# A graph layer with experts: row work of each bucket moved into the edge gather loop, buckets in order of edge count

## The chip, the cores and the metric

The kernel runs on one core of a Trainium2 chip. The metric is the device time of one execution in microseconds, the median of several runs. All arithmetic is fp32 where nothing else is said.

## What is computed

Cut to what matters, N = 6250 nodes, 100,000 edges, D = 256, 16 experts, the best 2 of them for each node:

```python
xn  = layernorm(x)
agg = segment_sum(xn[dst] * edge_weight[:, None], src, N)      # rows gathered by dst, summed by src
h   = relu((xn + agg) @ W1 + b1) @ W2 + b2                     # 256 -> 512 -> 256
k, v = per-head norm of xn (8 heads); kv = k^T v / N           # over all nodes
x2  = x + h + xn @ kv + xn
xn2 = layernorm(x2)
val, idx = top_k(xn2 @ gate_w + gate_b, 2); w = softmax(val)
moe = sum over the 2 of w * (relu(xn2 @ w1[idx] + b1[idx]) @ w2[idx] + b2[idx])
out = x2 + layernorm(xn2 + moe) * gamma + beta
```

## The kernel before, in words

Nodes lie in NT = 49 buckets of 128 rows. The program is a string of blocks, and all engines meet at the end of each.

1. Sorting (line 484 on). Edges are counted by bucket and group of edges (28 groups), the counts rounded up to quads of four edges, and each quad gets an address. Buckets lie one after another in their natural order; `base` is the first quad of each, by a scan over `bucket_quads`. VectorE builds matrices for each group (`matrices`), TensorE and ScalarE turn them into records, and GpSimd scatters the records to DRAM, eight scatters a group (line 594). At the end tables are made that say, for each *part*, which tile of 128 sorted edges it takes and which bucket it adds to.
2. The gather loop (line 1029 on). There are ET = 816 tiles of 128 edges. GpSimd gathers 128 rows of `xn` for each with an indirect DMA (line 1137) into one of 24 places, three batches of eight. SP puts the indices of a batch in place once the batch that had these places before is used up (`stage`, waiting for a count of sums `s_sum`), and tells TensorE when a batch has landed (`landed`). A part is one tile for one bucket; a tile at a boundary is used by two, so there are more parts than tiles, ST = 864. For each part VectorE builds a 128x128 matrix of edge weights (`build`, line 1246), 12 parts ahead, TensorE multiplies it with the gathered rows (line 1161) into one of SUMB = 4 PSUM banks, and VectorE adds the sum to the bucket's rows in `xh` (`add`, line 1255). TensorE's sum c waits for VectorE's add c - 4. The loop body is a `pair` of 48 parts. Beside the parts run, in rounds 1 to 7, the head norms and the products of all 49 buckets, seven buckets a round (`heads`: VectorE at parts 12, 24, 36 and 48, TensorE's products ahead of parts 40 to 46); in round 8 the kv matrix is finished; in rounds 9 to 15 attention's product is added to the residual (`attention`).
3. The row stage (line 1459 on): 49 buckets, two a loop body, software-pipelined over seven steps with two sets of buffers. For each: copy of h, transposes, the hidden product (line 1529), ReLU (line 1591), the second product (line 1547), `x2` (line 1640), layer norm, `x2b` and `xn2` stored by SP, gate product, top two, and the rank of each choice among those for the same expert (`hot`, `place`, `slot2`). GpSimd turns the slots into indices and scatters the node ids with two indirect DMAs a bucket (`step`, lines 1495 to 1508); step t waits until step t - 2 has landed. SP loads w1 at the start and w2 piece by piece.
4. A short block (line 1736 on) makes tables for the experts' tiles. GpSimd reads the dispatched ids back (line 1746). Then come the experts' tiles, 114 of them, and the final norm.

The two lines of the scatter on which much rests are these:

```python
if over(half):
    pool.wait_ge(s_idst[p], half * (16 * TOPK))     # the step two before has landed
```

Of the kernel before, what the change touches and what calls it, by code (L numbers as in the profile page):

```python
# [18 lines left out]
I32 = mybir.dt.int32  # L19
# [39 lines left out]
def gps_layer(nc, x, src, dst, edge_weight, gW1, gb1, gW2, gb2, klw, klb, vlw, vlb,  # L59
# [32 lines left out]
    ST = -(-(ET + NT - 1) // (2 * ROUND)) * 2 * ROUND  # L92
    EROUNDS = ET // ROUND
    LSTEP = 4
# [25 lines left out]
    with ctx:  # L120
# [21 lines left out]
        def carver(region, size):  # L142
            at = [0]

            def carve(words):
# [54 lines left out]
        match = [a.bitcast(BF16) for a in (carve(GT * EC // 2),  # L200
                                           xh[:, sort_at + EC + NBG:sort_at + EC + 3 * NBG])]
        assert GT * EC // 2 <= 2 * NBG and GT * NGRP <= 512 and NR % 2 == 1
# [20 lines left out]
        edge_sel = carve(ROUND * P)  # L223
        rec_rows = edge_sel[:, 0:BT * P * REC].rearrange("p (c s w) -> p c s w", c=BT, w=REC)
        nd = carve(GT * D)
        sq = carve(GT * D)
# [3 lines left out]
        assert BT * P * REC <= GT * D and 2 * ST <= GT * D  # L230
# [35 lines left out]
        base = kvt[:, 0:NT]  # L266
# [10 lines left out]
        xT = [carve(D) for _ in range(2)]  # L277
# [4 lines left out]
        col_f = carve(EC // 2)  # L282
        landed_row = col_f.bitcast(I32)[0:1, 0:BT * P // LSTEP]
        release_row = col_f.bitcast(I32)[0:1, BT * P // LSTEP:BT * P // LSTEP + P]
        assert BT * P // LSTEP + P <= EC // 2
        col_f = col_f.bitcast(BF16)
# [3 lines left out]
        carve = carver(arena, AW)  # L290
        hin = [carve(D) for _ in range(2)]
        hT = [carve(D) for _ in range(2)]
        g1 = [carve(H) for _ in range(2)]
        x2 = [carve(D) for _ in range(2)]
        x2b = [carve(D) for _ in range(2)]
        xn2 = [carve(D) for _ in range(2)]
        xn2T = [carve(D) for _ in range(2)]
        beta_row = carve(D)
        hot = [carve(TOPK * NX).rearrange("p (k e) -> p k e", k=TOPK) for _ in range(2)]
        hot_both = [carve(NX // 2).bitcast(BF16) for _ in range(2)]  # L300
        hot_sum = [carve(NX // 2).bitcast(BF16) for _ in range(2)]
        place = carve(NX)
        hot_place = carve(TOPK * NX).rearrange("p (k e) -> p k e", k=TOPK)
# [56 lines left out]
        top_f = [sb(f"top_f{i}", [P, TOPK]) for i in range(2)]  # L360
        slot2 = [sb(f"slot2_{i}", [P, TOPK]) for i in range(2)]
# [6 lines left out]
        dest_all = sb("dest_all", [P, XT])  # L368
        b1_tile = sb("b1_tile", [P, FC * XT])
# [6 lines left out]
        mv2 = [sb(f"mv2_{i}", [P, 2]) for i in range(2)]  # L376
        std2 = [sb(f"std2_{i}", [P, 1]) for i in range(2)]
# [106 lines left out]
        with nc.Block() as block:  # L484
# [55 lines left out]
            def _(pool):  # L540
# [13 lines left out]
                pool.iota(ids_all, pattern=[[P, NT], [NTP, TOPK]], base=0, channel_multiplier=1,  # L554
# [172 lines left out]
            def _(dve):  # L727
# [66 lines left out]
                dve.tensor_tensor_scan(tiles_f[:], ones[:, 0:NT], bucket_quads[:, 0:NT], 0.0, ALU.mult, ALU.add).then_inc(s_dve, 1)  # L794
                dve.wait_ge(s_dve, n.add())
                dve.tensor_tensor(base, tiles_f[:], bucket_quads[:, 0:NT], ALU.subtract).then_inc(s_dve, 1)
# [112 lines left out]

                rounds(0)  # L910
                at0 = n.n
# [38 lines left out]
                then(dve.tensor_reduce(tile_bucket[:], past, AX, ALU.add))  # L950
                dve.tensor_scalar(tile_bucket_i[:], tile_bucket[:], float(NT - 1), None, ALU.min).then_inc(s_bk, 1)
                past_sum(tile_f, off_step)
                then(dve.tensor_tensor(tile_f, parts, tile_f, ALU.subtract))
# [58 lines left out]
        s_xT = sem("xn_transposed")  # L1012
        s_xTe = sem("xn_transpose_copied")
        s_att = sem("attention_rows")
        s_res = sem("residual_rows")
# [1129 lines left out]
```

## Time and profile before

| | us |
|---|---|
| median of the runs | 2666.47 (2661.55 to 2671.39) |
| span of the profiled execution | 2663.8 |
| sorting | 0 to 618 |
| gather loop | 618 to 1691 |
| row stage and reading back the ids | 1691 to 2028 |
| experts and end | 2028 to 2664 |

Busy over the whole span: TensorE 1707 us (64%), GpSimd 1611 (60%), VectorE 1534 (58%), ScalarE 644 (24%). No engine is busy throughout, so each stretch has to be read by itself: which engine is busy in it, and what the others wait for. The profiled execution is 2.7 us shorter than the median of the runs.

### The profile page before, as it was taken

How to read it: one execution, taken by the hardware profiler on the slowest of the kernel's cores; microseconds unless marked ns; L12 is line 12 of the kernel's file. 1: busy time of each engine (PE TensorE's matmuls, PEld its weight loads, DVE VectorE, ACT ScalarE, POOL GpSimd, SP SyncE). 2: the span in 40 equal slices, each digit the busy share in tenths (PEclk: the TensorE clock that was granted, in tenths of full speed). 3: DMA queues.
4: the chain of work that ended last, by engine and by line, in shares of the span. 5: the costliest groups of instructions: out<-in, count | busy, mean ns of one | idle time of the engine just before them, and what ended most of it. 6: DMA issues, size and time to landing. Idle time of an engine off the chain costs nothing. (4 is left out here: it accounts for less than half of the span.)

```text
span 2663.8 us, 42526 instructions
## 1 busy us (share of the span) xinstructions
PE 1707.0 (64%) x8895; PEld 1423.3 (53%) x8896; DVE 1534.1 (58%) x4251; ACT 643.5 (24%) x1976; POOL 1610.9 (60%) x1802
## 2 busy tenths in 40 slices
PE   6406666624566666565566665798853999999900
PEld 2106666623455555454455454687843888888800
DVE  8598555534776666776566665365542343344477
ACT  4607555510000000000000000244421333333322
POOL 8006888876777777777777777033433555555535
PEclk9758777765678877878788877798976999999955
DMA  4001000134433333334443334643331111111175
GB/s 144 0 0 30 17 16 16 30 3 128 131 114 115 116 114 114 115 105 122 125 118 117 117 106 99 170 75 62 67 62 52 61 61 61 59 63 61 57 219 174
DMA packets 159628, 227.50 MB, mean 85 GB/s; under 512 B 51782, under 2 KB 118916, under 8 KB 159519
## 3 DMA queue, kind: packets, MB, share of 16 engines
q0 software_dynamic: 60816, 138.87, 18.7%
q1 hardware_dynamic: 85934, 74.74, 10.8%
q10 hardware_dynamic: 12768, 12.85, 1.5%
q14 instruction: 92, 0.75, 0.1%
q8 instruction: 18, 0.29, 0.1%
HBM read 182.97 MB, written 42.96 MB: 85 GB/s over the span
## 5 line engine op out<-in xcount | busy, mean ns | idle before, releaser
L1137 POOL DMA_INDIRECT lower<-xn_rows,lower x816 | 804.2, 986 | 254.6 <-issue 248.1
L1161 PE MATMUL bank<-lower 128*128 x1728 | 592.6, 503 | 387.9 <-SPq L1062 283.0
L1161 PEld LDWEIGHTS bank<-lower 128*128 128x128 f32 x1728 | 424.2, 258 | 528.3 <-issue 450.8
L1255 DVE TENSOR_TENSOR xh<-xh,bank 128x256 f32 x864 | 363.8, 421 | 289.9 <-PE bank L1161 283.7
L594 POOL DMA_INDIRECT edge_records_sorted<-lower x224 | 308.1, 1375 | 221.8 <-ACT lower L705 153.8
L1246 DVE TENSOR_SCALAR lower<-iota_n,lower 128x128 f32<-128x128 f32 x864 | 315.0, 366 | 87.0 <-issue 83.7
L638 PE MATMUL bank<-lower 128*64 128x128 f32 x1568 | 227.8, 319 | 112.8 <-ACT lower L689 110.1
L638 PEld LDWEIGHTS bank<-lower 128*64 128x64 f32 x1568 | 221.6, 167 | 117.4 <-DVE lower L893 110.8
L1861 POOL DMA_INDIRECT expert_rows<-arena,dest_idx x114 | 114.7, 1006 | 198.0 <-DVE arena L1957 187.2
L1891 PEld LDWEIGHTS bank<-arena 128*128 128x128 f32 x1824 | 223.6, 193 | 6.6 <-issue 0.8
L1948 DVE TENSOR_SCALAR arena<-bank,b_tile 128x128 f32<-128x128 f32 x456 | 128.4, 344 | 170.3 <-PE bank L1891 170.3
L1891 PE MATMUL bank<-arena 128*128 128x128 f32 x1824 | 224.3, 277 | 0.4 <-ACT arena L1929 0.4
L1912 PE MATMUL bank<-upper,arena 128*128 x912 | 223.8, 388 | 0.1
L689 ACT ACTIVATE lower<-lower 128x32 f32<-128x32 f32 x784 | 169.3, 309 | 123.6 <-DVE lower L878 123.3
L1912 PEld LDWEIGHTS bank<-upper,arena 128*128 128x128 f32 x912 | 163.9, 189 | 30.2 <-issue 6.4
L1929 ACT ACTIVATE arena<-lower 128x1024 f32 x114 | 120.5, 1057 | 61.0 <-issue 61.0
L1869 POOL DMA_INDIRECT arena<-xn_rows,tok_idx x114 | 109.5, 960 | 40.4 <-issue 33.4
L1107 ACT ACTIVATE arena<-bank 128x256 f32<-128x256 f32 x49 | 18.8, 384 | 458.8 <-PE bank L1186 458.8
L1506 POOL DMA_INDIRECT dispatched_ids<-slot_id,slot_idx x98 | 94.5, 964 | 53.8 <-POOL slot_id L1502 34.1
L1957 DVE COPY arena<-bank 128x256 f32<-128x256 f32 x114 | 48.4, 425 | 132.7 <-PE bank L1912 132.7
L1501 POOL CAST slot_idx<-slot 128x2 uint32<-128x2 f32 x49 | 9.7, 198 | 175.9 <-issue 77.0
L1529 PE MATMUL bank<-arena,upper 128*128 128x128 f32 x784 | 112.1, 302 | 3.5 <-ACT arena L1598 3.4
(290 smaller groups left out, 2330.5 us busy)
## 6 DMA issues: line engine op xcount, KB each, us to landing
lower<-xn_rows,lower POOLq DMA_INDIRECT x816
arena<-xn_rows ACTq DMA_DIRECT2D x14, 896.0 KB, 5.5
lower<-in_L_ffn_w SPq DMA_DIRECT2D x1, 8192.0 KB, 26.3
xn_rows<-xh SPq DMA_DIRECT2D x7, 896.0 KB, 4.2
x_plus_beta<-arena SPq DMA_DIRECT2D x49, 128.0 KB
xn_rows<-xh SPq DMA_DIRECT2D x49, 128.0 KB
upper<-in_x SPq DMA_DIRECT2D x1, 6144.0 KB
upper<-in_L_ffn_w SPq DMA_DIRECT2D x12, 512.0 KB
```

The source lines that it names most:

```text
L594: pool.indirect_dma_start(rec_dram, bass.IndirectOffsetOnAxis(quad_idx[i][:, c:c + 1], 0), quads[i][:, c * QW:(c + 1) * QW], None).then_in ...
L638: mm = pe.matmul(bank[6 + p][0:NQ * QW, 0:P], moving[p][:, e].rearrange("p c w -> p (c w)"), row_hot[p][:, e, :], start=e == 0, stop=e == ...
L689: done = act.activation(moving[p][:, e, :, 1], col_hot[p][:, e, :], ACT.Copy, scale=group_wgt[p][:, e:e + 1])
L1137: pool.indirect_dma_start(edge_rows[:, q * GB + c, :], None, xn_dram, bass.IndirectOffsetOnAxis(gath_idx[q].bitcast(U32)[:, c:c + 1], 0)). ...
L1161: pe.matmul(bank[c % SUMB][:, 0:D], edge_sel[:, c % ROUND, :], rows_flat[:, ds(places[c % GB] * D, D)], start=True, stop=True).then_inc(s_ ...
L1246: dve.tensor_scalar(edge_sel[:, c % ROUND, :], iota_n[:], lane[:, ds(t, 1)], weight_s[:, ds(t, 1)], ALU.is_equal, ALU.mult).then_inc(s_sel, 1)
L1255: dve.tensor_tensor(xh[:, at], xh[:, at], bank[c % SUMB][:, 0:D], ALU.add).then_inc(s_acc, 1)
L1861: pool.indirect_dma_start(y_dram, bass.IndirectOffsetOnAxis(dest_idx[p][:], 0), yrow[p], None).then_inc(s_yst[p], 16)
L1891: mm = pe.matmul(bank[2 + p][:, m * P:(m + 1) * P], w1_tile[p][:, c * F + m * P:c * F + (m + 1) * P], tokT[p][:, c * P:(c + 1) * P], start ...
L1912: mm = pe.matmul(bank[6 + p][:, 0:D], hidT[p][:, m * P:(m + 1) * P], upper[:, ds(e * (FC * D) + m * D, D)], start=False, stop=m == FC - 1)
L1929: act.activation(w1_tile[p], lower[:, ds(e * (DC * F), DC * F)], ACT.Copy).then_inc(s_w1t, 1)
L1948: dve.tensor_scalar(hidT[p][:, m * P:(m + 1) * P], bank[2 + p][:, m * P:(m + 1) * P], b1_tile[:, ds(t + m * XT, 1)], 0.0, ALU.add, ALU.max ...
```

## The change

- Sorting: buckets get a key of edge quads x 64 + their number, and a rank among these keys by comparing all with all (49x49). Their quads are laid out in rising order of count. After the first four groups, `bucket_order` works out which bucket stands at each place, and prepares the ids' table with it.
- The loop's body becomes a round of PER = 18 parts, and ST = 49 x 18 = 882. As buckets stand in rising order of size, the bucket at place s is complete when 18(s + 1) parts are added. SUMB becomes 3, `landed` is looked at every 3 parts, bucket and place numbers are loaded 6 at a time, matrices are built 9 parts ahead in 18 buffers. The heads' work of rounds 1 to 7 now lies beside 18 parts (VectorE at parts 1, 3, 6, 9 and 18, with the bias add of the residual in it; TensorE ahead of parts 11 to 17).
- The row stage as a block is gone. Its work is a `slot`, with one set of buffers: TensorE's `turn`, `hidden`, `second` (with attention's product added in PSUM), `turn_xn2`, `gate` and `ranks`, VectorE's `residual`, `norm`, `choose` and `placed`, and ScalarE's copies, ReLUs and root, which now also issues the load of xn and both stores. Rounds 9 to 16 hold two slots each, rounds 17 to 48 one, and the last slot runs after the loop.
- The slots of all buckets are kept in `slot_all`. The scatter of the ids is the same `step`, now at the start of the block that follows, before the ids are read back. w1 and w2 (8 MB each) are loaded at the start of that block too.

```diff
-    ST = -(-(ET + NT - 1) // (2 * ROUND)) * 2 * ROUND
+    PER = 18
+    ST = NT * PER
-    LSTEP = 4
+    LSTEP = 3
+    LB = 6
...
+                dve.tensor_tensor(by_bucket, bucket_key.unsqueeze(2).to_broadcast([P, NT, NT]),
+                                  bucket_key.unsqueeze(1).to_broadcast([P, NT, NT]), ALU.is_gt).then_inc(s_dve, 1)
...
+                dve.tensor_reduce(bucket_rank, by_bucket, AX, ALU.add).then_inc(s_dve, 1)
...
                 rounds(0)
+                bucket_order()
...
-        SUMB = 4
+        SUMB = 3
...
+                def slot(s):                                   # ScalarE
+                    b = bucket(s)
+                    act.wait_ge(s_acc, s * PER + PER)
+                    act.activation(hin, xh[:, ds(b * D, D)], ACT.Copy).then_inc(s_hin, 1)
+                    act.wait_ge(s_hT, s + 1)
...
+                    act.activation(hxT, bank[3][:, 0:2 * D], ACT.Copy).then_inc(s_hTe, 1)
...
+                def hidden(s):                                 # TensorE
+                    pe.wait_ge(s_hTe, s + 1)
...
+                def second(s):
+                    pe.wait_ge(s_gr, s * HC + HC)
...
+                ALONE = (0, 3, 6, 9, 12)
+                FIRST, OTHER = (0, 2, 4, 7, 8), (9, 11, 13, 16, 17)
...
+                with pe.Fori(TWO_FROM + 1, ONE_FROM) as r:
+                    two = (r - TWO_FROM) * 2
+                    parts(r, slot(two, FIRST) | slot(two + 1, OTHER))
+                with pe.Fori(ONE_FROM, NT) as r:
+                    parts(r, slot(r - 1, ALONE))
...
+                ALONE = (1, 7, 8, 13)                          # VectorE
+                FIRST, OTHER = (1, 5, 6, 9), (10, 14, 15, PER)
...
             @block.gpsimd                                      # the block after the loop
             def _(pool):
+                def step(j, k):
...
+                run_steps(pool, step, 0, NT - 1, 1, (NT - 1) // 2)
+                for p in range(2):
+                    pool.wait_ge(s_idst[p], 16 * TOPK * ((NT + 1 - p) // 2))
                 pool.wait_ge(s_block, 1)
```

## Rows read from the trace of the kernel before

**Rows 1.** Busy time by stretch: us and instructions of each engine, clock, DMA

```profile
618.00:1691.00 1073.00, 675.66 (x2329) 522.59 (x2327) 692.76 (x1898) 33.94 (x70) 804.15 (x816) 0.77 0.40 113
1691.00:2028.00 337.00, 249.75 (x1669) 226.81 (x1669) 158.61 (x897) 127.57 (x442) 110.51 (x196) 0.86 0.37 83
2028.00:2664.00 636.00, 469.58 (x3083) 418.12 (x3083) 297.64 (x922) 195.29 (x293) 322.43 (x485) 0.88 0.29 91
```

Columns of the above: stretch, its length, then TensorE matmul, weight load, VectorE, ScalarE and GpSimd.

**Rows 2.** Groups of instructions, gather loop: busy and mean, idle before with releaser

```profile
L1137 POOL DMA_INDIRECT lower<-xn_rows,lower x816 | 804.2, 986 | 254.6 <-issue 248.1 <-DMA lower<-lower 6.5
L1161 PE MATMUL bank<-lower 128*128 x1728 | 592.6, 503 | 387.9 <-SPq L1062 283.0 <-DVE lower L1246 54.8 <-DVE xh L1255 49.1
```

**Rows 3.** By line: duration min, median and max in ns, first and last start

```profile
L1137 POOL DMA_INDIRECT lower<-xn_rows,lower x816: 941/946/2737, 618.0 to 1670.2; - x164
...
L1255 DVE TENSOR_TENSOR xh<-xh,bank x864: 406/422/423, 632.1 to 1690.4; 128x256 f32 x173
...
L1506 POOL DMA_INDIRECT dispatched_ids<-slot_id,slot_idx x98: 954/960/1181, 1729.8 to 2010.5; - x98
```

**Rows 4.** GpSimd in order of time, end of the scatter: start, us, instruction

```profile
1999.11 0.18 POOL L1501 CAST slot_idx<-slot 128x2 uint32<-128x2 f32 x1 [3.10 <-DMA dispatched_ids<-slot_id,slot_idx]
...
2001.48 0.96 POOL L1506 DMA_INDIRECT dispatched_ids<-slot_id,slot_idx  x1 [0.30 <-DMA dispatched_ids<-slot_id,slot_idx]
...
2008.10 0.18 POOL L1501 CAST slot_idx<-slot 128x2 uint32<-128x2 f32 x1 [1.92 <-issue]
```

**Rows 5.** Waits in the row stage: who waited for whom, us, times, longest

```profile
DVE slot L1675 <- POOL slot_id L1502: 48.2, 20, 5.9
...
POOL slot_idx L1501 <- DMA dispatched_ids<-slot_id,slot_idx: 39.3, 16, 5.3
...
DVE arena L1640 <- issue: 3.0, 3, 1.2
```

**Rows 6.** VectorE in order of time, first parts of a heads round

```profile
816.97 0.35 DVE L1246 TENSOR_SCALAR lower<-iota_n,lower 128x128 f32<-128x128 f32 x1 [4.23 <-issue]
...
818.52 0.42 DVE L1255 TENSOR_TENSOR xh<-xh,bank 128x256 f32 x1
...
819.15 0.42 DVE L1255 TENSOR_TENSOR xh<-xh,bank 128x256 f32 x1
...
822.79 0.35 DVE L1246 TENSOR_SCALAR lower<-iota_n,lower 128x128 f32<-128x128 f32 x1 [0.48 <-issue]
...
825.52 2.01 DVE L1280 TENSOR_REDUCE arena<-arena 128x56 f32<-128x1792 f32 x1
...
829.82 0.34 DVE L1246 TENSOR_SCALAR lower<-iota_n,lower 128x128 f32<-128x128 f32 x1
```

**Rows 7.** TensorE in order of time, sums between the products of the heads

```profile
866.19 0.59 PE L1161 MATMUL bank<-lower 128*128 x2
...
867.50 0.59 PE L1161 MATMUL bank<-lower 128*128 x2
```

**Rows 8.** Groups of instructions, row stage

```profile
L1529 PE MATMUL bank<-arena,upper 128*128 128x128 f32 x784 | 112.1, 302 | 3.5 <-ACT arena L1598 3.4
...
L1547 PE MATMUL bank<-upper,arena 128*128 128x256 f32 x392 | 94.1, 383 | 0.0
...
L1591 ACT ACTIVATE arena<-bank,gb_col 128x128 f32<-128x128 f32 x196 | 56.0, 369 | 29.5 <-PE bank L1529 22.8 <-remote 4.8
```

**Rows 9.** GpSimd in order of time, during the centring of a heads round

```profile
828.13 2.59 POOL L1137 DMA_INDIRECT lower<-xn_rows,lower  x1 [0.30 <-issue]
```

**Rows 10.** VectorE and GpSimd in order of time, sorting

```profile
117.39 1.59 DVE L810 TENSOR_TENSOR upper<-xh 128x1372 f32<-128x1372 f32 x1
...
119.12 2.66 DVE L815 TENSOR_TENSOR xh<-xh,upper 128x1372 f32<-128x1372 f32 x1
...
219.04 1.44 POOL L594 DMA_INDIRECT edge_records_sorted<-lower  x1 [153.84 <-ACT lower L705]
...
257.06 0.17 DVE L903 CAST lower<-lower 128x8 uint32<-128x8 f32 x1 [8.31 <-DMA edge_records_sorted<-lower]
```

More of the change, by code:

```diff
@@ L1120, in _ @@
                 heads(NG - 1)
-                with act.Fori(0, NG - 1) as g:
-                    attention(g)
-                attention(NG - 1)
+                act.wait_ge(s_kv, DC)
+                act.dma_start(beta_row, row(beta)).then_inc(s_beta, 16)
+                load_xn(bucket(0))
+                slot(0)
+                with act.Fori(1, NT - 1) as s:
+                    slot(s)
+                slot(NT - 1)
+                act.wait_ge(s_x2st, 16 * NT)
+                act.wait_ge(s_xn2st, 16 * NT)
             @block.gpsimd
@@ L1208, in _, with slot @@
+                def slot(s, places):
+                    steps = turn, hidden, second, turn_xn2, gate
+                    return {c: [lambda f=f: f(s)] for c, f in zip(places, steps)}
+                ALONE = (0, 3, 6, 9, 12)
+                FIRST, OTHER = (0, 2, 4, 7, 8), (9, 11, 13, 16, 17)
                 pe.wait_ge(s_srec, 16 if ET % P == 0 else 32)
@@ new lines, in norm @@
+                def norm(s):
+                    if over(s):
+                        dve.wait_ge(s_x2st, s * 16)
+                    dve.tensor_tensor(x2b, x2, beta_row, ALU.add).then_inc(s_x2b, 1)
+                    dve.wait_ge(s_std2, s + 1)
+                    then(dve.reciprocal(rstd2[:], std2[:]))
+                    if over(s):
+                        dve.wait_ge(s_xn2k, s)
+                        dve.wait_ge(s_xn2st, s * 16)
+                    dve.tensor_scalar(xn2, x2, mv2[:, 0:1], rstd2[:], ALU.subtract, ALU.mult).then_inc(s_xn2, 1)
+                    dve.wait_ge(s_xn2, s + 1)
@@ new lines, in _, with slot @@
+                bucket_now = [None]
+                per_slot = 9
+                def slot(s, places, last=True):
+                    steps = [lambda: placed(s - 1)] if over(s) else [lambda: None]
+                    steps += [lambda: residual(s), lambda: norm(s), lambda: choose(s)]
+                    return {c: [f] for c, f in zip(places, steps)}
+                ALONE = (1, 7, 8, 13)
+                FIRST, OTHER = (1, 5, 6, 9), (10, 14, 15, PER)
+                constants()
+                parts(TWO_FROM, slot(0, FIRST) | slot(1, OTHER))
@@ new lines, in _ @@
+                with dve.Fori(TWO_FROM + 1, ONE_FROM) as r:
+                    n.enter(r - TWO_FROM - 1, 2 * per_slot)
+                    two = (r - TWO_FROM) * 2
+                    parts(r, slot(two, FIRST) | slot(two + 1, OTHER))
+                    n.leave(ONE_FROM - TWO_FROM - 1)
+                with dve.Fori(ONE_FROM, NT - 1) as r:
+                    n.enter(r - ONE_FROM, per_slot)
+                    parts(r, slot(r - 1, ALONE))
+                    n.leave(NT - 1 - ONE_FROM)
+                parts(NT - 1, slot(NT - 2, ALONE))
@@ L1450, in gps_layer @@
+                placed(NT - 2)
+                residual(NT - 1)
+                norm(NT - 1)
+                choose(NT - 1)
+                placed(NT - 1)
+        s_w1 = sem("w1_loaded")
+        s_w2 = sem("w2_loaded")
         s_ids = [sem(f"ids_staged{i}") for i in range(2)]
         s_idst = [sem(f"ids_landed{i}") for i in range(2)]
[L1453 to L1456 removed]
```

684 lines of the change are left out of this document (278 added, 406 removed).

## Prediction, as recorded before the changed kernel was measured

> **What bounds the kernel now.** I read the busy time by stretch first [rows 1]. The program is a string of blocks: sorting the edges (0 to 618 us), the gather loop (618 to 1691), the row stage (MLP, norm, gate, ids; 1691 to 2028 where the first dispatched ids are read back), and the experts and the end (636 us), which the change doesn't touch. In the gather loop GpSimd is the busiest engine: 816 indirect gathers [rows 2]. One takes 0.946 us, the gap behind it 0.30, so 1.25 us [rows 2, 3], and 816 of them 1020 us of the 1073. The rest is mostly 21 gathers of up to 2.7 us, each under a 2 us VectorE operation on 1792 elements, like the one of 2.59 us at 828 [rows 9]. So this loop waits for gathers, and VectorE and TensorE have room.
>
> The row stage isn't what its engines suggest. TensorE is busy 250 of 337 us, but GpSimd's scatter of the ids sets the pace: VectorE waits 48 us for it before overwriting a slot buffer, and GpSimd itself waits for landings [rows 5]. A step (two casts, two scatters) waits until the step two before it has landed. The step at 2008.10 follows the scatter issued at 2001.48 by 6.62 us, and the same parity's step at 1999.11 by 8.99 us [rows 4]. Nothing else was moving then, so 4.5 us a bucket is the scatter's own pace; 49 of them are 220 us. This is the row to keep in mind: the change moves this scatter out from behind the work it ran beside.
>
> **The change, part by part.** *Sorting.* Before the first scatter of edge records at 219.04 VectorE has no pause, so what is added there counts in full [rows 10]. Two comparisons or products over 49x49 = 2401 elements and a third, and two reductions over as many: an operation of 1372 elements took 2.66 us there with transposed operands and 1.59 without, and 1792 elements took 2.01 in the loop [rows 6, 10]; so about 2.7 each, four of them, 11 us with the small ones. The second group (`bucket_order`, 10 us) comes where VectorE later waits 8.31 us for a landing [rows 10]; I leave 5 us of it, also for GpSimd held up by long VectorE operations, and 1 for the tables. Sum +17 (bounds 11 and 22).
>
> *The row stage goes away, the scatter stays.* From 337 us to: 220 for 49 steps with nothing beside them, about 20 because 16 MB of weights now load in the first part of it, 7 for the last landing. That is 247, a gain of 90 only. Bounds: 3.33 us a step if no landing were waited for (2.37 us from cast to second scatter plus 0.96) [rows 4], 163 + 27 = 190; and the pace of before with traffic beside it, (2008.10 - 1729)/48 = 5.8 a step, 285 + 7 = 292, where the 1729 is the first scatter [rows 3].
>
> The Trainium skill (DMA: Bandwidth & Descriptors, Anatomy of one DMA — SWDGE (gpsimd) path) gives such a transfer a fixed cost of about 2.0 us, most of it the write receipt. By that the landing would be in time and the step would cost what its issue costs, 163 us in all; the trace's 6.62 us doesn't agree, and the measurement decides.
>
> *The gather loop.* Its VectorE and TensorE now have to do, per 18 parts, what the rows below say, while GpSimd needs for the 17 tiles behind them 17 x 1.25 = 21.2 us (25.1 in a round with three held gathers). The engines are in order and coupled: TensorE may be three sums ahead of VectorE's adds, so a wait on one side soon stops the other. Costs, each from a row:
> - a part, when data lies ready: 819.15 - 818.52 = 0.63 us on VectorE [rows 6]; 18 are 11.3. Register loads 0.48 and more, three a round, 1.5 [rows 6].
> - a heads round (7). Its VectorE work was spread over 48 parts and now has 18: bias add 2.0, centring 829.82 - 825.52 = 4.3, squares 2.0, scaling 2.9, adding up 0.9: 12.1. Eleven parts 7.0, loads 1.0. The last seven parts each stand behind TensorE's products of the heads: 867.50 - 866.19 = 1.31 a part [rows 7], 9.2. Sum 29.3.
> - a bucket's row work. VectorE was busy 158.6/49 = 3.2 us for a bucket [rows 1]; its 17 operations now each wait for the one before (0.06, an estimate), and a register load: 4.7. TensorE and ScalarE: hidden product 112.1/49 = 2.3, four ReLUs 56.0/49 = 1.14, second product 94.1/49 = 1.9 [rows 8], attention about 0.6 (four of hidden's sixteen). These 5.9 us are serial, with a single set of buffers, and TensorE's sums queue behind them.
> - a round with one bucket (32). 11.3 + 1.5 + 4.7; the bucket's last add, ScalarE's copy, four transposes and the first sum before VectorE adds again, 2.1 idle; adds held behind hidden and second product (5.9 and two sums against four adds, `placed` and a load), 2.4. Sum 22.0, against GpSimd's 21.2. No cover is left.
> - a round with two buckets (8): 11.3 + 1.5 + 9.4 + 2 x 3.1 (now only two parts stand between the products) + 2 x 1.7 (after `choose` TensorE does ranks and transposes before the next sum). Sum 32.
>
> Chain from 618: 44 until the first round and the bias split are done (as before, but the adds no longer catch up), 7 x 29.3 = 205, the round with the kv matrix 20, waiting for beta 4, 8 x 32 = 256, 32 x 22 = 704, the last bucket alone 16. That is 1249 against 1073, +176. Behind a late add waits the release of a gather buffer on SP, and behind that GpSimd: three batches of eight tiles let it run ahead once, not every round. Bounds: +38 if GpSimd sets the pace all along (18 more parts and the last bucket, 22 + 16), and +280: a bucket round at 24.5 and a double one at 36, since the clock was 0.77 of full speed in this loop [rows 1] and the products of a bucket were priced at 0.86.
>
> *Sum* against the profiled execution: 2664 + 17 + 176 - 90 = 2767. The median of the runs is 2.7 us above that execution's span, so 2770.
>
> **Rivals.** *The gather still sets the pace.* For it: VectorE's own work is 17.5 of 21.2 us in most rounds, GpSimd is the bound now, and a few us can be absorbed. Against: the double and heads rounds exceed 21 by VectorE's work alone. Time 2664 + 17 + 38 - 90 = 2629, which is not slower. It decides if a round of one bucket stays under 21.2 us and the 15 others lose little.
>
> *The scatter is issue-bound.* For it: in steps without other waits GpSimd goes on after 3.33 us. It decides if landings take under 6.66 - 2.37 = 4.3 us after the second scatter. Against: 6.62 in a quiet stretch. Time 2770 - 57 = 2713. The skill's rule above leads here.
>
> *Each turn of the loop costs 4 us.* At every turn of the 48-part loops VectorE stood 4.2 us with nothing to wait for [rows 6], hidden so far. There were some 12 such turns; now there would be 45, 190 us, and the time 2960. Against: in the row stage, a loop of shorter body, VectorE's issue gaps before its first operation reach only 1.2 us [rows 5], and 18 parts with two buckets are shorter than 48 parts with one group. The Trainium skill (Runtime: NRT & Kernel Launch, Instruction fetch mechanics) says that a taken branch stalls when its target is outside the current two-page window. By it the shorter body would be free, the trace agrees as far as these rows go.
>
> **How the numbers follow.** My forecast 0.70, with its own range 2700 to 2870. The gather keeping the pace 0.14 (2620 to 2700). Issue-bound scatter with a bound loop 0.05. The 4 us turns 0.06. Gather keeping the pace and a short scatter together, 2572: 0.05. The range of 2640 to 2870 leaves out the last two, a part of the second, and little of the first. More than 2% away from before, about what a measurement can tell from no change, is under 2613 or over 2720. Faster 0.06; same 0.20 (second case, third case, edge of the first); slower 0.74.
>
> **What would show it.** Right: GpSimd's gathers no longer 1.25 us apart in the first third of the loop, idle before a gather on a landing of its index batch; the last gather at 1830 or later instead of 1670; ScalarE's last bucket near 1885; casts of the scatter alternating 3.3 and 5.7 us for 220 to 260 us with the other engines idle. Wrong: the last gather near 1690; double rounds under 26 us; a scatter step of 3.3; VectorE idle on issue of 4 us in each round. The single weakest term is the round with one bucket: 1 us there is 32 us.

## The result, and the profile after

The changed kernel takes **3030.3 us** (3028.6 to 3032.1) against 2666.5: 1.136 times the time before, 95% interval 1.130 to 1.142. In a second sitting it was 3065.6 against 2709.3, 1.132 (1.127 to 1.138). The forecast was 2770 with a range of 2640 to 2870: the direction was right, the size was not.

First the same table by stretch as [rows 1], of the kernel after: sorting, gather loop with the row work in it, the block that scatters the ids, and the rest. The columns are the start and end, the length, busy us of each engine with instructions, the granted clock of TensorE, DMA share and GB/s.

```profile
core 0: us, PE busy (x) PEld busy (x) DVE busy (x) ACT busy (x) POOL busy (x), PEclk, DMA share, GB/s
0.00:632.00 632.00, 315.08 (x1817) 258.94 (x1819) 405.52 (x552) 286.88 (x1171) 375.59 (x306) 0.73 0.15 33
632.00:2117.00 1485.00, 1020.75 (x4031) 774.71 (x4030) 884.93 (x2818) 169.01 (x462) 798.54 (x816) 0.77 0.32 90
2117.00:2390.00 273.00, 1.30 (x6) 0.71 (x6) 4.23 (x21) 1.53 (x2) 109.30 (x196) 0.50 0.34 62
2390.00:3030.00 640.00, 469.84 (x3079) 418.24 (x3079) 295.59 (x914) 195.16 (x292) 322.64 (x485) 0.88 0.28 87
```

Against [rows 1] that is +14 for sorting, +412 for the loop, 337 turned into 273, -64, and +4 for the rest. The forecast had +17, +176, -90 and 0. So nearly all of the error, 236 of 263 us, is in one term, the loop. No engine is full in it: TensorE is busy 69% of the stretch, VectorE 60%, GpSimd 54%.

The page's group of the gathers shows that they no longer set the pace; compare the idle time before them in [rows 2]. The two sources after it are the register loads of VectorE and TensorE (min/median/max in ns; the columns otherwise as in [rows 3]).

```profile
L1231 POOL DMA_INDIRECT lower<-xn_rows,lower x816 | 798.5, 979 | 620.2 <-DMA lower<-lower 385.3
```

```profile
L1395 DVEq TENSOR_LOAD <-upper x147: 805/1071/1558, 637.5 to 2091.2; - x147
L1242 PEldq TENSOR_LOAD <-arena x147: 824/1470/1848, 634.5 to 2089.3; - x147
```

GpSimd stands still for 385 us waiting for its index batches, which SP stages only when sums have released a buffer. The same load in the kernel before was this:

```profile
L1262 DVEq TENSOR_LOAD <-upper x108: 593/598/854, 623.6 to 1684.8; - x108
```

**The loop round by round**, measured from the first add of a round to that of the next, against the working on record:

| part of the loop | forecast | measured |
|---|---|---|
| until the second round's first add | 44 | 46.0 |
| 7 heads rounds | 7 x 29.3 = 205 | 7 x 30.9 = 216.5 |
| round with the kv matrix, waiting for beta | 24 | 21.5 |
| 8 rounds with two buckets | 8 x 32 = 256 | 8 x 39.0 = 311.9 |
| 32 rounds with one bucket | 32 x 22.0 = 704 | 869.9 (27.2 each) |
| last bucket | 16 | 19.6 |

The one-bucket round is 166 of the 236 us that were missed, the two-bucket round 56, the heads 11. Below, "one-bucket round" is the mean of 29 of the 32 (27.3 here) and "two-bucket round" the mean of six of the eight (39.2), which leaves out the first and the last of each kind.

Where a one-bucket round changes over, in order of time, VectorE, TensorE and ScalarE (GpSimd's and part of the weight loads' lines are left out):

```profile
1770.30 0.42 DVE L1388 TENSOR_TENSOR xh<-xh,bank 128x256 f32 x1
1770.86 0.42 ACT L1178 ACTIVATE lower<-xh 128x256 f32 x1 [9.48 <-DVE xh L1388]
...
1771.33 0.57 PE L1287 MATMUL bank<-ident,lower 128*128 128x128 f32 x2 [1.46 <-ACT lower L1178]
...
1771.69 0.63 PE L1290 MATMUL bank<-ident,lower 128*128 128x128 f32 x2
...
1772.43 0.35 DVE L1379 TENSOR_SCALAR lower<-iota_n,lower 128x128 f32<-128x128 f32 x1 [1.71 <-issue]
...
1773.26 2.92 PE L1255 MATMUL bank<-lower 128*128 x6 [0.94 <-DVE lower L1379]
...
1774.62 0.42 DVE L1388 TENSOR_TENSOR xh<-xh,bank 128x256 f32 x1 [1.84 <-PE bank L1255]
...
1778.89 1.47 PE L1255 MATMUL bank<-lower 128*128 x6
```

The last add of a bucket (1770.30) starts ScalarE's copy; TensorE stood waiting for the copy, transposes, then does its own register load (0.83 us) and the first sum, and only at 1774.62 does VectorE add again: 4.3 us from add to add, where two adds are 0.63 apart with data ready [rows 6]. One of VectorE's own register loads, 1.42 us, lies inside these 4.3. The three sums take 2.92 us here, at a granted clock of 0.50 of full speed (the 1.2 GHz level) after TensorE's wait, and 1.47 a few us later at 1.00 (2.4 GHz), after the 3 us of the hidden product.

The row of waits for VectorE over those 29 rounds (1256.6 to 2048.0; us, times, longest) says how the time is spent beside its 16.1 us of work a round:

```profile
DVE xh L1388 <- PE bank L1255: 168.9, 168, 3.1
DVE lower L1379 <- issue: 99.1, 87, 1.7
DVE lower L1554 <- issue: 12.8, 29, 0.4
```

That is 5.8 us a round for sums, and 3.4 us without a releaser at the builds, 87 times in 29 rounds. Three register loads stand in each round, and at 0.82 and 1.41 us in turn they are 3.35. So that idle time is the loads. The other 1.9 us of the 27.3 are short gaps between dependent operations, a further register load (0.44) among them.

### The profile page after: what moved, and what is told of

Its sections match the earlier page's. It is cut to its first block and busy times, and to the rows that moved or that the text cites. A ratio compares the mean times of both kernels' runs of the same rounds, so it can differ in the third digit from the quotient of the medians.

```text
span 3030.3 us, 43604 instructions
## 1 busy us (share of the span) xinstructions
PE 1807.0 (60%) x8931; PEld 1452.6 (48%) x8932; DVE 1590.3 (52%) x4303; ACT 652.6 (22%) x1927; POOL 1606.1 (53%) x1802
## 5 line engine op out<-in xcount | busy, mean ns | idle before, releaser
L1255 PE MATMUL bank<-lower 128*128 x1764 | 632.2, 496 | 209.1 <-DVE lower L1379 81.7
L1255 PEld LDWEIGHTS bank<-lower 128*128 128x128 f32 x1764 | 390.7, 241 | 355.8 <-issue 298.7
L1388 DVE TENSOR_TENSOR xh<-xh,bank 128x256 f32 x882 | 371.1, 421 | 324.4 <-PE bank L1255 321.6
L1867 ACT ACTIVATE arena<-bank 128x256 f32<-128x256 f32 x114 | 43.8, 384 | 553.3 <-PE bank L1833 553.2
L1297 PEld LDWEIGHTS bank<-lower,upper 128*128 128x128 f32 x784 | 145.6, 276 | 9.7 <-ACT lower L1182 1.1
L1297 PE MATMUL bank<-lower,upper 128*128 128x128 f32 x784 | 139.1, 353 | 0.7 <-ACT lower L1182 0.7
```

The source lines that it names most:

```text
L1255: pe.matmul(bank[c % SUMB][:, 0:D], edge_sel[:, c % ESEL, :], rows_flat[:, ds(places[c % LB] * D, D)], start=True, stop=True).then_inc(s_s ...
L1297: mm = pe.matmul(bank[4][:, m * P:(m + 1) * P], gW1_sb[:, c, m * P:(m + 1) * P], hxT[:, c * P:(c + 1) * P], start=c == 0, stop=c == DC - 1)
L1388: dve.tensor_tensor(xh[:, at], xh[:, at], bank[c % SUMB][:, 0:D], ALU.add).then_inc(s_acc, 1)
```

## The experiments

All are variants of the changed kernel, or of the kernel before, and each ran beside the kernel before on one chip, in one sitting. Sittings differ: the median of the kernel before was 2666, 2700, 2709, 2668 and 2668 us in five of them (2709 and the last 2668 on one and the same chip, at different times) and 2979 in a sixth. So totals are compared as ratios, or by their rounds. The loop without row work, the two banks, the doubled hidden product and the kernel before repeated were executed once each, so they are read by their rounds and stages alone. The changed kernel repeated is the measure for that:

> The changed kernel itself, unchanged, as the measure for its variants on one chip: 3025 to 3060 us, 1.12 to 1.145 times the kernel before.

It took 3065.6 us; its one-bucket round was 27.29 and its two-bucket round 39.3, as at first. Its ids block and the sorting are what is longer. So round times can be compared between these sittings, the sixth left out.

### The loop without row work

```diff
-                with pe.Fori(ONE_FROM, NT) as r:
-                    parts(r, slot(r - 1, ALONE))
+                with pe.Fori(TWO_FROM, NT) as r:
+                    parts(r)
+                ...
+                with pe.Fori(1, NT) as s:
+                    for f in (turn, hidden, second, turn_xn2, gate):
+                        f(s)
```

> The changed kernel with the row work taken out of the gather loop: the loop sums the buckets in the new order, in rounds of 18 tiles, and the MLP, norm and gating of the 49 buckets run one after another behind it. What it tells is the time of a round without row work, and the length of one bucket's chain alone. Theory A (the row work on VectorE and TensorE is what a round of the changed kernel waits for): rounds without it take 21.6 to 23.5 us, which is 17 to 18 gathers at 1.25 plus the register loads, against 27.3; so 4 to 6 us a round are the price of one bucket's row work. Rival B (the loop itself is slower in rounds of 18 with loads of 6, the row work costs little): rounds without row work take 25 us or more. A bucket's chain alone: 14 to 18 us, so the total is near 3030 - 170 + 49 x 16 = 3640.

The total is 3516.7 us; a round took 21.6 us. The group of the gathers over those rounds (1110 to 1737):

```profile
L1231 POOL DMA_INDIRECT lower<-xn_rows,lower x499 | 473.8, 950 | 152.1 <-issue 152.1
```

No gather waits for anything: 1.25 us each, as before. So rounds of 18, new order and slow loads all fit under GpSimd, and the row work alone is what lengthens a round, by 5.7 us for one bucket and 17.6 for two. Theory A holds. Summing the buckets in another order costs these rounds nothing by itself. A bucket's chain alone, behind the loop, takes 16.3 us, as expected; the total stayed under the 3640 expected because the loop lost 326 us and not 170.

### The register loads

```diff
-                                place_row[0:1, ds(r * PER + c, LB)]
+                                place_row[0:1, ds(r * (PER // LB * 8) + c // LB * 8, 8)]
```

(the same for `bucket_row`, and the tables are laid out so by their DMAs)

> The changed kernel with the two tables of the register loads laid out in places of 8: each load of VectorE and of TensorE takes 8 values from a 32-byte aligned address, as in the kernel before, in place of 6 values from 24-byte steps. Nothing else differs in what is computed. Theory A (the loads, in series with the adds on both engines, made the gather loop longer than the sum): each load takes 0.60 us instead of 0.82 and 1.41 to 1.47, which is 1.5 us a round on each engine; 49 rounds x 1.5 = 75 us off the changed kernel if one engine's loads are in series, 150 off if both are. Rival B (the loads lie beside other waits, and the surplus is in dependent operations and a slow TensorE): less than 20 us off. Rival C (the address does not matter, the number of values does): the loads of 8 take 1.5 us or more, and the total does not fall.

```profile
L1400 DVEq TENSOR_LOAD <-upper x147: 594/600/866, 644.4 to 2049.5; - x147
L1247 PEldq TENSOR_LOAD <-arena x147: 587/595/971, 641.3 to 2048.2; - x147
```

Eight aligned values load in 0.60 us, less than six unaligned ones, so it isn't their number. 3020.2 us against 3065.6 in the same sitting, -45. The one-bucket round went from 27.3 to 26.05, the two-bucket round only from 39.3 to 38.9. That is between A and B: 1.25 of the 1.5 us that one engine saves, and nothing for the second. Over the same 29 rounds VectorE's idle time at the builds fell from 99.1 to 56.1 us, 1.48 a round, and its waits for sums rose from 168.9 to 175.8, 0.24 a round. So the loads of the two engines stand beside each other, not in series.

### The turn of the bucket

```diff
-                ALONE = (0, 3, 6, 9, 12)
+                ALONE = (2, 5, 8, 11, 14)
```

(and VectorE's places from 1, 7, 8, 13 to 3, 9, 10, 15)

> The changed kernel, but in a round with one bucket its five steps on TensorE stand before parts 2, 5, 8, 11, 14 and VectorE's before 3, 9, 10, 15, instead of 0, 3, 6, 9, 12 and 1, 7, 8, 13. So the first two sums of a round no longer stand behind the bucket's copy on ScalarE and its transposes. Theory A (the turn of the bucket, 4.3 us from the last add of a round to the first sum's add in the trace, is an idle of both engines that this place makes): 1 to 2 us a round off, 31 rounds, the total 30 to 60 us under the changed kernel's. Rival B (the engines are full, the wait only moves to a later place): less than 0.5 us a round, total within 15 us.

2939.2 us, ratio 1.102 (1.099 to 1.104) against 1.136: -91 us. The one-bucket round is 24.5, 2.8 less, more than theory A gave, and VectorE's waits for sums in 29 rounds fell from 168.9 to 79.9 us, 3.1 a round. The two sums ahead of the turn are enough:

```profile
1250.03 0.67 PE L1287 MATMUL bank<-ident,lower 128*128 128x128 f32 x2
1250.23 0.42 DVE L1388 TENSOR_TENSOR xh<-xh,bank 128x256 f32 x1
...
1250.86 0.42 DVE L1388 TENSOR_TENSOR xh<-xh,bank 128x256 f32 x1
1250.91 1.93 PE L1255 MATMUL bank<-lower 128*128 x6
...
1252.12 0.42 DVE L1388 TENSOR_TENSOR xh<-xh,bank 128x256 f32 x1 [0.58 <-PE bank L1255]
```

VectorE adds at 1250.23 and 1250.86 while TensorE transposes and goes on to the next sums; its wait for a sum in these rows is 0.58, where it was 1.84 behind a wait of 1.71.

This could be the place among the parts, or the dependence on the bucket finished an instant ago. The next one keeps the places and takes the dependence away:

```diff
-                    parts(r, slot(r - 1, ALONE))
+                    parts(r, slot(r - TWO_FROM, ALONE))
```

(one bucket a round, finished nine rounds before; the last nine follow the loop one by one)

> The changed kernel, but every round from the ninth on takes one bucket, the one finished nine rounds earlier, and the nine last buckets come one after another behind the loop. The steps stand at the same parts (0, 3, 6, 9, 12 and 1, 7, 8, 13). Theory A (in the changed kernel the first sum of a round stands behind the copy and the transposes of the bucket whose last add has just been made; 2.8 us of a round are this dependence): with a bucket that is long finished such a round takes 24.0 to 25.0 us at the old places, as it did with the later places. Rival B (the place of the steps among the parts mattered, not the dependence): 26.5 to 27.5. The nine buckets alone take 14.9 us each, 134, against the 8 rounds with two buckets that go, 8 x (39 - 24.5) = 116; total by A 2945 to 2965, by B 3030 to 3060 (a chip like the first).

> One bucket a round, finished nine rounds earlier, the steps at the old parts, once more, on a chip where the landings of gathers don't hold the loop. Theory A (2.8 us of a changed kernel's round are the wait for the bucket just finished): rounds with one bucket take 24.0 to 25.0 us. Rival B (the place of the steps among the parts mattered, not the dependence): 26.5 to 27.5.

The first of these ran, like three others below, in the sitting where the kernel before took 2979 us. Transfers came late there all through the loop: GpSimd waited 488 us for its index batches, up to 20 at a time, against 155 us in the run of the same kernel below, and its rounds took 25 to 42 us. Which transfer was late first I did not settle. Its 3277.9 us against 2979.4 (1.103) tells nothing of the dependence. The second ran in a sitting like the others: 2933.2, ratio 1.099, and every one-bucket round took 23.1 to 24.7 us, 23.9 in the mean, at the old places. VectorE's waits for sums in 29 rounds are 71.2 us instead of 168.9, 3.4 a round. So it is the dependence: 3.4 us of a round were the wait for the bucket just finished and the slower products behind it.

TensorE's clock follows. The rows are the one-bucket rounds of the changed kernel, of the turn made later, and of the bucket of nine rounds before, with the same work in each:

```profile
1256.60:2048.00 791.40, 564.22 (x2205) 428.87 (x2204) 467.97 (x1596) 91.06 (x261) 466.95 (x493) 0.80 0.35 96
```

```profile
1250.20:1961.60 711.40, 519.11 (x2210) 390.87 (x2209) 463.17 (x1597) 91.66 (x262) 469.70 (x495) 0.84 0.39 107
```

```profile
1134.90:1827.30 692.40, 502.60 (x2206) 379.58 (x2205) 463.88 (x1595) 91.06 (x261) 468.68 (x495) 0.88 0.39 110
```

The same 2205 products keep TensorE busy 564, 519 and 503 us, at a granted clock of 0.80, 0.84 and 0.88. VectorE's busy time stays at 464 to 468. A part of what a wait costs is that the products behind it run at the lower clock, as the 2.92 us against 1.47 for three sums showed.

### Is TensorE in series?

```diff
-                    for m in range(HC):
+                    for m in (*range(HC), *range(HC)):
```

(the hidden product of each bucket is done twice into the same bank)

> The changed kernel with the hidden product of each bucket done twice into the same bank (16 more matrix products of 128x128 a bucket, the result is the same). They take 2.6 us in the loop's trace. Theory A (a bucket's products on TensorE are in series with the sums, no slack is left there): rounds with one bucket 29.7 to 30.0 instead of 27.3, with two 44 instead of 39, and the total grows by 110 to 130 us. Rival B (VectorE is what a round waits for, TensorE has slack): less than 1 us a round, total +40 at most.

The total is 3131.0 us. One-bucket round 29.2, +1.9; two-bucket round 44.4, +5.1. Against the 2.6 us that theory A took for the added product this looks like three quarters in the one and all in the other. But the added work has to be read from the trace: the hidden product's busy time grew by 62.2 us in 29 one-bucket rounds, 2.1 each, and by 25.3 in six two-bucket rounds, 4.2 each, where the sums also got slower (granted clock 0.73 instead of 0.76). So the product is nearly wholly in series in both. That is A, though 29.2 lies just under its 29.7.

```diff
-        SUMB = 3
+        SUMB = 2
```

> The changed kernel with two PSUM banks for the sums of parts in place of three, so TensorE can be two sums ahead of VectorE's adds. Theory A (VectorE's idle time on sums, 5.7 us of a 27.3 us round with one bucket, is sums held behind a bucket's products, and the depth of the banks covers part of each hold): each of the four holds in a round shows one add more, 0.6 to 1 us each, so such a round takes 29.5 to 31 us and the total grows by 70 to 120 us. Rival B (the depth does not matter, both engines are simply full): under 0.5 us a round, total within 20 us.

The total is 3127.0 us. One-bucket round 29.9, +2.6; two-bucket round 39.9, +0.7. For one bucket the lead of TensorE over the adds covers part of each hold, as A says: VectorE's waits for sums in 29 rounds grew from 168.9 to 237.8 us, 2.4 a round. How much of that is the lead alone isn't shown, because the granted clock fell from 0.80 to 0.73 with it and TensorE's busy time grew by 2.5 us a round. For two it hardly matters, so another thing rules there.

### The two-bucket round

In the trace of the three edits together (next part) I read the waits over six such rounds, 12 buckets:

```profile
DVE xh L1392 <- PE bank L1259: 72.1, 47, 2.5
...
PE bank L1318 <- DVE lower L1573: 37.7, 12, 3.4
PE bank L1283 <- DVE lower L1590: 28.7, 12, 2.6
```

Each engine waits for the other in turn. For each bucket TensorE waits 3.1 us at its fourth step (transposing xn2) for VectorE's norm, and 2.4 us at the ranks for VectorE's choice of the bucket before, though it is only the *next* bucket's transposes that are held there. That one can be moved:

```diff
                 def turn(s):
-                    if over(s):
-                        ranks(s - 1)
                 ...
                 def hidden(s):
+                    if over(s):
+                        ranks(s - 1)
```

(VectorE reads the ranks two or three parts later)

> The kernel with the three edits together (aligned loads, scatter without waits, bucket's steps two parts later), and one edit more: TensorE does the ranks of the bucket before with the next bucket's hidden product instead of ahead of its transposes, and VectorE reads them two parts later. Theory A (a round with two buckets, 38.6 us, is a chain that goes back and forth between TensorE and VectorE; 2.5 us of TensorE's idle time stand twice in it at the ranks, which wait for the choice of the bucket before): 3 to 5 us off each of the 8 rounds, 25 to 40 in all. Rival B (such rounds are full on TensorE's side, the wait moves): less than 1 us a round.

> The three edits together and the ranks done with the next hidden product, once more on another chip. Theory A (the ranks' wait for the choice of the bucket before stands twice in the chain of a two-bucket round): these rounds take 34 to 36 us instead of 38.6. Rival B (the wait moves): 37.5 or more.

In the sitting with late transfers 3113.5 against 2979.4 (1.047), undecided. In the other 2741.6, ratio 1.029 (1.026 to 1.032), against 1.035 for the three edits without it. The one-bucket round is 23.5 there, 0.5 longer; the two-bucket round went from 38.9 to 35.1, and the wait at the ranks is gone from the answer; the one for the norm stands:

```profile
DVE xh L1392 <- PE bank L1259: 48.8, 40, 3.5
...
PE bank L1318 <- DVE lower L1573: 37.6, 12, 3.4
```

So A holds for these rounds, 3.9 us off where it gave 3 to 5, but about half of the gain is lost again in the 32 one-bucket rounds, and the total fell by less than the 25 to 40 us it gave. 3 us still part 35.1 from the forecast's 32. The waits for the norm, 3.1 us twice a round, are more than that; whether they are the cause was not tried.

### The edits together

> The changed kernel with three edits together: loads of 8 aligned values, the ids scattered without waits for landings, and the bucket's steps two parts later in rounds with one bucket. Theory A (each acts on its own stretch, so the gains add up): 45 + 120 + 30 to 60 off, a total of 2800 to 2870, 1.035 to 1.06 times the kernel before, which it does not reach. Rival B (the loop falls back to the gather's pace once loads and turn are mended, 21.4 us a round): 2700 or less.

The total is 2759.0 us, ratio 1.035 (1.032 to 1.037), 271 us under the changed kernel. One-bucket round 23.0: the loads' 1.25 and the turn's 2.8 add up, as A says. The total lies between A's range and B's, 41 us under A, since A had put the turn at 30 to 60 us and it gave 91 alone. The gather's pace of 21.4, rival B, isn't reached.

> One bucket a round, finished nine rounds earlier, with aligned loads, the scatter without waits and the ranks done with the next hidden product. Theory A (with the turn's wait and the slow loads gone a round is near the gather's pace of 21.4 us): rounds of 21.4 to 22.5 us and a total of 2700 to 2740, still above the kernel before. Rival B (the bucket's products keep 1.5 us a round above the gather): rounds of 23 and a total of 2750 to 2770.

> One bucket a round, finished nine rounds earlier, with aligned loads, the scatter without waits and the ranks done with the next hidden product, once more on another chip. Theory A (with the turn's wait and the slow loads gone a round is near the gather's pace of 21.4 us): rounds of 21.4 to 22.5 and a ratio of 1.01 to 1.03 to the kernel before. Rival B (the bucket's products keep a round 1.5 us above the gather): rounds of 23 and a ratio of 1.03 to 1.04.

In the sitting with late transfers 3175.5 (1.066). In the other 2748.0, ratio 1.030 (1.028 to 1.033), with rounds of 22.7 (VectorE's first place is 4 in both, not 1): one us above the loop without row work, between the theories and nearer to B.

### The scatter of the ids

```diff
-                    if over(half):
-                        pool.wait_ge(s_idst[p], half * (16 * TOPK))
-                    pool.tensor_copy(slot_idx[p][:], slot_all[:, ds(t * TOPK, TOPK)])
+                pool.tensor_copy(slot_i[:], slot_all)
+                for j in range(NJ):
+                    pool.indirect_dma_start(..., IndirectOffsetOnAxis(slot_i[:, j:j + 1], 0), ids_all[:, j:j + 1], None)
```

> The changed kernel with the ids scattered at once: one cast of all slots, then the 98 indirect DMAs one behind the other with no wait for those before, from columns that stay. Theory A (each pair of steps waits for two landings, so the wait is the bound of the block): what is left is GpSimd's issue, near 1.26 us each as for the gathers, 98 x 1.26 = 124 plus about 15 for the last landing; the block goes from 273 to about 145 and the total to about 2900. Rival B (the DMA rings work off such scatters one behind the other at the pace seen, 2.4 us each quiet and 3.9 beside the weights): the block stays over 230 and the total over 2990.

```profile
2129.20 0.96 POOL L1662 DMA_INDIRECT dispatched_ids<-arena,dest_all  x1 [0.30 <-issue]
2130.46 0.95 POOL L1662 DMA_INDIRECT dispatched_ids<-arena,dest_all  x1 [0.30 <-issue]
...
2266.08 1.15 POOL L1667 DMA_INDIRECT arena<-dispatched_ids,arena  x1 [18.54 <-DMA dispatched_ids<-arena,dest_all]
```

Scatters follow each other every 1.26 us and the block, from the cast to the reading back, takes 142.7 us instead of 273: 2909.7 us, ratio 1.077 (1.075 to 1.080). Theory A. The queue takes scatters 1.26 us apart even beside the weights. The edit also takes away the two casts of each step and the wait for them, and a step with these and without a wait for landings takes 3.3 us [rows 4]. So of the 4.76 us of a quiet step 1.4 were the wait for landings, of the 7.7 us beside the weights 4.4, and 0.8 us of each step were the casts.

> The changed kernel, but the two big weight loads wait for the end of the ids scatter. Theory A (the loads of 16 MB stretch each landing while they last: 7.7 us a step against 4.76 after them): all 49 steps take 4.8, the scatter ends after 235 us in place of 267, and the expert stage then waits some 48 us for its first weights; the total moves by +5 to +25 us (3035 to 3055). Rival B (the first steps were slow for another reason, as the code's first passes): the first 12 steps stay at 7.7 us, and the total is 3070 or more.

The weight loads now wait for the scatter's end. The cast of the first bucket, of the 13th and of the 49th, in the changed kernel:

```profile
2117.75 0.19 POOL L1665 CAST slot_idx<-node_all 128x2 uint32<-128x2 f32 x1 [72.99 <-POOLq L1097]
...
2210.07 0.19 POOL L1665 CAST slot_idx<-node_all 128x2 uint32 x1 [0.51 <-DMA dispatched_ids<-slot_id,slot_idx]
...
2381.57 0.19 POOL L1665 CAST slot_idx<-node_all 128x2 uint32<-128x2 f32 x1 [0.47 <-DMA dispatched_ids<-slot_id,slot_idx]
```

and with late weights:

```profile
2123.86 0.19 POOL L1667 CAST slot_idx<-node_all 128x2 uint32<-128x2 f32 x1 [72.06 <-POOLq L1097]
...
2190.50 0.19 POOL L1667 CAST slot_idx<-node_all 128x2 uint32 x1
...
2379.72 0.18 POOL L1667 CAST slot_idx<-node_all 128x2 uint32<-128x2 f32 x1
```

The first 12 steps took 7.7 us each beside the weights and 5.55 without them, the 36 others 4.76 and 5.26, which is the sitting (the changed kernel repeated had 8.5 and 5.2 in its own). So the weights make a step some 3 us longer while they load. Total 3067.7, ratio 1.136: the steps came out as A says, though slower by the sitting, and the total above its 3055. Weights that start later cost what the scatter gains.

### The kernel before without these waits

> The kernel before, with only the waits of its own ids scatter on the landings of two tiles earlier taken away, by a place of its own for each tile's slots. Theory A (the row stage of the kernel before, 337 us, was itself paced by the scatter's landings, 5.8 us a tile beside TensorE's 4.5): the stage takes about 54 steps x 4.5 = 245 us, and the total is 2570 to 2590. Rival B (the stage is paced by the chain through four engines, the scatter runs beside it): within 15 us of 2666.

> The kernel before without the scatter's waits on landings once more, on the chip of the runs beside it. Theory A (the scatter's landings pace its row stage wherever it runs, and how much depends on the chip): 15 to 50 us less than the kernel before, which makes it the fastest of all. Rival B (the first gain was of that one chip): no difference beyond 0.3%.

2654.2 us, ratio **0.983** (0.980 to 0.986), and in the sitting with late transfers 2939.6, ratio 0.985 (0.980 to 0.991). This version beats both kernels, by a little under 2%. One of the two casts of a step went with the waits, so the gain isn't of the waits alone. The gain of 46 us is half of what A said: with the scatter out of the way the row stage takes 5.4 us a bucket, not TensorE's 4.5. GpSimd now waits for VectorE's slots, 99 us in 260, so another engine sets the pace; which link of its chain does I did not settle. The kernel before, profiled again in another sitting, shows that the gain depends on that:

> The kernel before itself, unchanged, for a profile from the chip on which the runs beside it are made. Both theories: the same stages as in its first profile within 1.5%.

```profile
1742.19 1.01 POOL L1506 DMA_INDIRECT dispatched_ids<-slot_id,slot_idx  x1 [0.84 <-POOL slot_id L1502]
...
2051.84 0.95 POOL L1506 DMA_INDIRECT dispatched_ids<-slot_id,slot_idx  x1 [0.30 <-issue]
```

First to last scatter 309.7 us here. By [rows 3, 4] it was about 280 at first; without the waits it was this:

```profile
1740.41 1.04 POOL L1500 DMA_INDIRECT dispatched_ids<-arena,dest_all  x1 [0.44 <-POOL dest_all L1497]
...
2000.01 0.96 POOL L1500 DMA_INDIRECT dispatched_ids<-arena,dest_all  x1 [0.30 <-issue]
```

That is 259.6 us. So 20 to 50 us of the row stage were waits for landings, the cast included. The profiled kernel before took 2712.0 us, as in the other runs of that sitting.

## Why the prediction was wrong, step by step

- **The bound of the kernel before** was read rightly: 1.25 us a gather sets the loop's pace, and it does so again (21.6 us a round) once the row work is out. The scatter's landings did hold the row stage, as [rows 5] said, but what was hidden behind them was 5.4 us a bucket rather than 4.5.
- **Sorting**, +17: measured +14.
- **The row stage leaves, the scatter stays**, -90: measured -64. The mechanism was right. The term mis-sized is a step beside the weights, 7.7 us where the sum had 4.5 and 20 us for all of them (12 steps, +18), and 4.76 for the quiet pair's 4.5 (36 steps, +9).
- **The loop**, +176: measured +412. The failed step is "a round with one bucket, 22.0". By VectorE's time, over the 29 rounds:

  | in a one-bucket round | in the sum | measured |
  |---|---|---|
  | VectorE's own work | 11.3 + 3.2 = 14.5 | 16.1 |
  | gaps between a bucket's operations, and its register load | 1.5 | 1.9 |
  | the three register loads of the parts | 1.5 | 3.4 |
  | idle until a sum is there | 2.1 + 2.4 = 4.5 | 5.8 |
  | all | 22.0 | 27.3 |

  The loads were priced at 0.5 each from a row of the kernel before, where eight aligned values were loaded; six values at 24-byte steps took 0.82 and 1.41, and aligning them gave 1.25 us a round back. The turn of the bucket was given 2.1 us, added up as single operations. It holds both engines at once for 4.3 us (a register load included), leaves TensorE at the lower clock, and empties the lead of sums that would have covered the next product; moving it gave 2.8 us back, taking the dependence away 3.4. No variant tested the first two rows, 2.0 of the 5.3 us, and no run shows the 0.06 us by which one operation was said to wait for the one before. The loads and the moved turn together bring the round from 27.3 to 23.0, but these 4.3 us are not all error, since 2.1 us for the turn were in the 22.0. The rounds of 23.0, and of 22.7 in the best variant, stay 1 us and more over the 21.6 without row work; what makes that up is open.
- **The bounds.** 24.5 us for such a round was meant for the clock alone and was too low, and with it the upper end of the range; by its own terms, 2.5 us in 32 rounds and 4 in 8, that end adds up to +288 and not +280. The lower end, +38, counted 22 us for 18 more parts at the gather's pace, though 816 gathers stay 816. In a sum of VectorE's work plus idle pieces each wait that is not foreseen only adds.
- **A round with two buckets, 32**: measured 39. The sum put the products behind VectorE's work and saw one direction of waiting. In fact the chain of a bucket goes from one engine to another fifteen times, and in a two-bucket round both engines wait in turn. 3.9 us were TensorE waiting at the ranks for the choice, in order in its queue ahead of work that was ready; the rest of the 7 stays open.
- **Heads rounds**, 29.3: measured 30.9, 5% off; no variant tested their terms.
- **Rivals.** *The gather still sets the pace*: false as the change stands, GpSimd waits 385 us; true without row work. *The scatter is issue-bound*: false, a step took 4.76 and more; it becomes true when nothing waits, 1.26 us apiece. In the trace of the changed kernel a scatter landed 1.8 us after its issue at the least, 6.3 in the median and 16.9 at the most. The rule of the Trainium skill that I weighed there (DMA: Bandwidth & Descriptors, Anatomy of one DMA — SWDGE (gpsimd) path), a fixed cost of about 2.0 us, fits the shortest of these and not the median. *Each turn of the loop costs 4 us*: false. VectorE's idle time on issue at the builds is 3.4 us in a round, and three register loads account for 3.35 of it. The turn itself shows at the branch: in the kernel before VectorE's next instruction came 3.0 us after it, in loop bodies of 320 and 326 instructions of the trace, and in the changed kernel 0.24 us after it, in bodies of 158 and 201. The Trainium skill (Runtime: NRT & Kernel Launch, Instruction fetch mechanics) has a taken branch stall when its target is outside the current two-page window; the traces, with the stall at the long bodies alone, agree.

## What to carry to other kernels

When work is moved into a loop whose engines run in order, don't price it as work to be added on one engine: follow its chain across the engines and add, at each hand-over, what stands in both queues behind the waiting instruction. Give the moved step an operand that has long been ready (another round's), or put a few independent instructions ahead of it, and wait for a result only where it is used. And where a scatter or gather in a loop waits for landings to reuse a tiny index buffer, give every step its own columns.

## What the runs showed of the hardware that I had not expected

- A register load's time hangs on its address as well as on the number of values: 8 values at 32-byte steps 0.60 us, 6 values at 24-byte steps 0.82 and 1.41 in turn on VectorE, 0.83 and 1.47 on TensorE, one value 0.3.
- The granted clock differs with waits of a few us: with the same products it was 0.80, 0.84 and 0.88 of full speed in the mean as the waits of a round grew shorter, and TensorE's busy time 564, 519 and 503 us.
- A loop's turn cost VectorE 3.0 us behind the branch with 320 instructions in the body, and 0.24 us with 158.
- Sittings differ in landings. The quiet scatter step was 4.76 us in one and 5.2 to 5.3 in two others; in one sitting late transfers made each kernel 11 to 16% longer than in its other sitting; and one chip gave 2709 us once and 2668 another time.
